# Three-layer graph network on one core: column chunks of 448, 448 and 458 behind the first pass, and two late bank drains in the plan

## The reference

```
gc(h, W, b) = adj @ (h @ W) + b
h  = maximum(layernorm(x), 0)
h  = relu(gc(h, W1, b1))        # W1 512 x 1024
h  = relu(gc(h, W2, b2))        # W2 1024 x 1024
out = x + gc(h, W3, b3)         # W3 1024 x 512
```

## Time and profile before

| what | us |
|---|---|
| median of 3 runs | 1581.48 |
| lowest and highest run | 1580.51 and 1583.2 |
| the profiled execution, its own time | 1582.09 |
| its span, first to last instruction | 1580.3 |
| PE busy | 1570.7 (99%) |
| DVE, ACT, POOL busy | 866.1, 644.3, 527.8 |
| mean granted clock of TensorE | 0.999 |

### The profile page before, as it was taken

The page is one execution under the profiler, slowest core; times in us unless marked ns, Lnnn a source line. Parts: engine busy times, 40 slices in busy tenths (PEclk is TensorE's granted clock), DMA queues, the critical chain, the costliest instruction groups (busy, mean ns, idle before and its releaser), DMA issues.

```text
span 1580.3 us, 21103 instructions
## 1 busy us (share of the span) xinstructions
PE 1570.7 (99%) x7638; PEld 1353.5 (86%) x7638; DVE 866.1 (55%) x1360; ACT 644.3 (41%) x1145; POOL 527.8 (33%) x488
## 2 busy tenths in 40 slices
PE   9999999999999999999999999999999999999999
PEld 7888889988878888989898989888898888888898
DVE  8983433256452456353545444764565536676766
ACT  5542222233343333342333333533455536555555
POOL 5863544346664544000000003573302333021302
PEclk9999999999999999999999999999999999999999
DMA  6966657555687888554557567783544357898887
GB/s 240 334 221 213 219 179 222 179 158 154 198 265 259 268 278 280 148 168 125 190 156 221 167 208 235 257 278 116 182 123 131 94 163 244 252 320 267 256 274 224
DMA packets 211091, 334.52 MB, mean 212 GB/s; under 512 B 25608, under 2 KB 96896, under 8 KB 210988
## 3 DMA queue, kind: packets, MB, share of 16 engines
q1 hardware_dynamic: 171484, 239.78, 49.1%
q0 software_dynamic: 15680, 55.31, 10.8%
q10 hardware_dynamic: 23824, 38.10, 6.9%
HBM read 243.75 MB, written 89.36 MB: 211 GB/s over the span
## 4 chain that ended last, share of the span: by engine, by line
PE 89%; DVE 4%; DMA 3%; ACT 2%; ACTq 1%; issue 0%; DVEq 0%; SPq 0%
PE ps L1818 29%; PE ps L1819 29%; PE ps L1820 29%; DVE ring L1449 2%; PE ps L1908 1%; PE ps L1907 1%; DMA raw<-adjT 1%; DMA raw<-HX 1%; DVE pair_buf L1491 1%; ACT pair_buf L1245 1%; DMA raw<-TS 1%; DVE even L1496 0%; ACT ring L1200 0%; DMA raw_tail<-adjX 0%; PE ps L1856 0%
## 5 line engine op out<-in xcount | busy, mean ns | idle before, releaser
L1449 DVE TENSOR_TENSOR ring<-raw,ring 128x512 fp32r<-128x512 f32 (+1 forms) x522 | 376.8, 738 | 409.6 <-ACT ring L1200 408.0
L1200 ACT CAST ring<-raw 128x512 fp32r<-128x512 f32 (+1 forms) x564 | 319.9, 576 | 489.4 <-PE ps L1820 373.4
L1818 PE MATMUL ps<-slots,still 128*128 128x512 f32 (+1 forms) x504 | 183.2, 364 | 1.5 <-DVE still L1397 1.0
L1819 PE MATMUL ps<-slots,still 128*128 128x512 f32 (+1 forms) x504 | 183.1, 363 | 0.0
L1820 PE MATMUL ps<-slots,still 128*128 128x512 f32 (+1 forms) x504 | 183.0, 363 | 0.0
L1818 PE MATMUL ps<-ring,even 128*128 128x512 f32 (+1 forms) x480 | 175.2, 365 | 2.5 <-DVE ring L1449 2.5
L1820 PE MATMUL ps<-ring,even 128*128 128x512 f32 (+1 forms) x480 | 175.0, 365 | 0.0
L1819 PE MATMUL ps<-ring,even 128*128 128x512 f32 (+1 forms) x480 | 174.9, 364 | 0.0
L1818 PE MATMUL ps<-ring,S 128*128 128x512 f32 (+1 forms) x420 | 153.1, 365 | 0.9 <-DVE ring L1449 0.9
L1819 PE MATMUL ps<-ring,S 128*128 128x512 f32 (+1 forms) x420 | 152.8, 364 | 0.0
L1820 PE MATMUL ps<-ring,S 128*128 128x512 f32 (+1 forms) x420 | 152.8, 364 | 0.0
(11 more groups left out here) (160 smaller groups left out, 3012.8 us busy)
## 6 DMA issues: line engine op xcount, KB each, us to landing
raw<-TS SPq DMA_DIRECT2D x160, 256.0 KB, 3.3
raw<-adjT SPq DMA_DIRECT2D x122, 256.0 KB, 3.9
raw<-adjT SPq DMA_DIRECT2D x41, 512.0 KB, 4.7
TS<-made SPq DMA_DIRECT2D x20, 1024.0 KB, 6.7
raw<-TS SPq DMA_DIRECT2D x80, 165.0 KB, 2.8
raw<-HS SPq DMA_DIRECT2D x50, 256.0 KB, 3.0
raw<-P SPq DMA_DIRECT2D x44, 256.0 KB, 4.2
HS<-pair_buf POOLq DMA_DIRECT2D x20, 512.0 KB, 4.8
```

The lines of the kernel that those rows point to most:

```text
L1200: act.copy(hi, src).then_inc(hi_done, 1)
L1449: dve.tensor_tensor(lo, src, hi.bitcast(F32), ALU.subtract).then_inc(lo_done, 1)
L1818: pe.matmul(out, st_hi, mv_hi, start=start, stop=False)
L1819: pe.matmul(out, st_hi, mv_lo, start=False, stop=False)
```

## The change

Two things are changed. First, `WIDTH` and `START` are doubled: the first pass keeps 512, 512 and 330 under the names `WIDTH1` and `START1`, with helpers `columns1`, `nodes1` and `within1`, and all later stages get 448, 448 and 458. Second, the planner puts off the "block" steps of the last two h1 blocks by 3 and 5 cuts instead of 2 (`LATE_BLOCKS`).

```diff
-WIDTH = (512, 512, 330)
-START = (0, 512, 1024)
+WIDTH1, WIDTH = (512, 512, 330), (448, 448, 458)
+START1, START = (0, 512, 1024), (0, 448, 896)
...
+LATE_BLOCKS = (3, 5)
...
-def columns_chunk(block):
+def columns_chunk(block, start):
...
-    return max(sum(c % HALF >= a for a in START) - 1 for c in range(first, last + 1))
+    return max(sum(c % HALF >= a for a in start) - 1 for c in range(first, last + 1))
...
-            p.later(lag, emit(g, j))
+            p.later({20: LATE_BLOCKS[0], 21: LATE_BLOCKS[1]}.get(j, lag), emit(g, j))
...
-            return slots1[:, j.slot, part, a, 0:WIDTH[c]]
+            return slots1[:, j.slot, part, a, 0:WIDTH1[c]]
...
+    def columns1(half, c):
+        return slice(half * STRIDE + START1[c], half * STRIDE + START1[c] + WIDTH1[c])
...
-                sp.dma_start(TS[t, :, :, within(c)], made[:, i % 2, :, 0:WIDTH[c]]).then_inc(made_stored[i % 2], 16)
+                sp.dma_start(TS[t, :, :, within1(c)], made[:, i % 2, :, 0:WIDTH1[c]]).then_inc(made_stored[i % 2], 16)
...
-                    need = columns_chunk(j.block) + 1
+                    need = columns_chunk(j.block, START1) + 1
...
-                    need = columns_chunk(j.block)
+                    need = columns_chunk(j.block, START)
```

More of the change, by code:

```diff
@@ L744, in slot1 @@
         if j.slot < RING1:
-            return slots1[:, j.slot, part, a, 0:WIDTH[c]]
-        return slots0[:, j.slot - RING1, part, a, 0:WIDTH[c]]
+            return slots1[:, j.slot, part, a, 0:WIDTH1[c]]
+        return slots0[:, j.slot - RING1, part, a, 0:WIDTH1[c]]
     def stage(s):
@@ L759, in within, with nodes1, within1 @@
         return slice(START[c], START[c] + WIDTH[c])
+    def columns1(half, c):
+        return slice(half * STRIDE + START1[c], half * STRIDE + START1[c] + WIDTH1[c])
+    def nodes1(half, c):
+        return slice(half * HALF + START1[c], half * HALF + START1[c] + WIDTH1[c])
+    def within1(c):
+        return slice(START1[c], START1[c] + WIDTH1[c])
     with ExitStack() as ctx:
@@ L950, in _ @@
                 if j.a is not None:
-                    src = adjT[j.block * P:(j.block + 1) * P, columns(j.a, j.chunk)]
-                    sp.dma_start(raw1[:, j.raw % RAW1, j.a, 0:WIDTH[j.chunk]], src)                         .then_inc(first_half_in if j.a == 0 else raw1_in[j.raw % RAW1], 16)
+                    src = adjT[j.block * P:(j.block + 1) * P, columns1(j.a, j.chunk)]
+                    sp.dma_start(raw1[:, j.raw % RAW1, j.a, 0:WIDTH1[j.chunk]], src)                         .then_inc(first_half_in if j.a == 0 else raw1_in[j.raw % RAW1], 16)
                     if j.a == 1:
@@ L962, in _ @@
                     for r in range(3):
-                        sp.dma_start(raw_tail[r * STEP:r * STEP + TAIL, :, 0:WIDTH[j.chunk]],
-                                     src[:, :, within(j.chunk)]).then_inc(tail1_in, 16)
+                        sp.dma_start(raw_tail[r * STEP:r * STEP + TAIL, :, 0:WIDTH1[j.chunk]],
+                                     src[:, :, within1(j.chunk)]).then_inc(tail1_in, 16)
                     continue
@@ L975, in _ @@
                     src = adjT[j.block * P:(j.block + 1) * P, :].rearrange("p (a n) -> p a n", a=2)
-                    sp.dma_start(raw1[:, r, :, 0:WIDTH[j.chunk]], src[:, :, within(j.chunk)]) \
+                    sp.dma_start(raw1[:, r, :, 0:WIDTH1[j.chunk]], src[:, :, within1(j.chunk)]) \
                         .then_inc(raw1_in[r], 16)
@@ L1124, in cut1 @@
             def cut1(j):
-                w = WIDTH[j.chunk] if j.chunk is not None else None
+                w = WIDTH1[j.chunk] if j.chunk is not None else None
                 if j.kind == "x":
@@ L1219, in _ @@
                             act.wait_ge(group_done, i + 1)
-                            act.copy(stage(s)[:, 0:WIDTH[c]], ps[:, 2 * m, 0:WIDTH[c]]).then_inc(copied, 1)
+                            act.copy(stage(s)[:, 0:WIDTH1[c]], ps[:, 2 * m, 0:WIDTH1[c]]).then_inc(copied, 1)
                             act.wait_ge(copied, 4 * c + m + 1)
@@ L1223, in _ @@
                             act.wait_ge(drained, 4 * c + m + 1)
-                        act.dma_start(P1[m, :, nodes(a, c)], stage(s)[:, 0:WIDTH[c]]) \
+                        act.dma_start(P1[m, :, nodes1(a, c)], stage(s)[:, 0:WIDTH1[c]]) \
                             .then_inc(stage_stored[s], 16)
@@ L1464, in _ @@
                     dve.wait_ge(group_done, i + 1)
-                    dve.tensor_copy(stage(s)[:, 0:WIDTH[c]], ps[:, 2 * m + 1, 0:WIDTH[c]]).then_inc(drained, 1)
+                    dve.tensor_copy(stage(s)[:, 0:WIDTH1[c]], ps[:, 2 * m + 1, 0:WIDTH1[c]]).then_inc(drained, 1)
             for kind, a in steps:
@@ L1585, in make @@
                 c, n = divmod(i, PAIRS)
-                w = WIDTH[c]
+                w = WIDTH1[c]
                 a, b = chunks1[c][2 * n], chunks1[c][2 * n + 1]
```

## The result

| | before | after |
|---|---|---|
| median, us | 1582.34 (4 runs) | 1597.8 (4 runs) |
| lowest and highest run | 1580.51 and 1584.9 | 1596.17 and 1599.19 |
| the profiled execution, its own time | 1582.09 | 1596.17 |
| its span | 1580.3 | 1594.4 |

The ratio is 1.0099, with a 95% interval from 1.0086 to 1.0112: slower by 15.5 us, where 5.5 us of gain were forecast. Of the rivals, 4 is the nearest.

What follows compares the result with a forecast made beforehand. PE, busy for 99% of the span, was taken as the bound. The terms 0 - 4.3 - 2.4 + 0.6 + 0.5 sum to -5.6 us, giving a forecast of 1576.0 us, own range 1574.5 to 1577.5.

Steps and rivals of the forecast that it cites:

- rival 4: The 448 lies off the straight line, a price step of 3.3 to 6.7 ns: 1587 to 1598 us; chance 0.05.
- Part 1: Matmuls of pass2, w2 and pass3, priced linearly by width: -90.4 and +90.6 us, together nothing within 0.5 us.
- rival 1: The 458 costs 3.3 ns more throughout, by the 330's dear pattern: +5.6 us, 1581.6; chance 0.09.
- Part 2: Pass2's begin: later drains remove PE's waits and the half clock, -4.6 us, leaving a 0.3 us wait: -4.3 us.
- Part 3: Pass3's last chunk: at 458 columns no waits on low parts and no dear 330 starts: -2.4 us.
- The cheaper pattern: Pass3's last chunk: the 458 at 203.9 ns, without the 3.3 ns extra of the 330 behind a wait.
- Part 4: First two chunks: shorter tiles cover loads less, 0.4 us in pass3, 0.2 in w2's first chunk: +0.6 us.
- Part 5: Kernel's end: the last DVE addition and store get 458 columns instead of 330: +0.5 us.
- Rivals 2 and 3: 2: loads not covered in narrower chunks, +2.5 us, chance 0.15; 3: late drains only move pass2's wait, +3 us, chance 0.05.

Runs made afterwards that it cites:

- the late drains alone: Against the kernel before, only the last two h1 blocks' later drains, all stages at 512, 512 and 330: 1578.97 us against 1581.91, ratio 0.9982.

## Why the prediction was wrong, step by step

**Part 1, the widths, "nothing within 0.5 us": wrong, and this is the failed step.** "I take the straight line, since two widths 182 columns apart lie on it with the same remainder" priced the 448 at 199.8 ns and the 458 at 203.9. They cost 202.7 and 208.3. Against before, the two chunks gain 3360 x (202.67 - 226.67) = -80.6 us, the third loses 1680 x (208.33 - 150.0) = +98.0, and the dear stretch adds 0.9: +18.2 (17.9 above was counted from the forecast's rounded prices). The bound named for the 448, 3.3 ns, held; the one for the 458, 3.3 ns too, did not (4.4). Two points always lie on a line, and their common remainder was no test of one. The rows had a warning in them, the 330's two prices 3.3 ns apart, which shows that the distance is set by something besides the columns; I used it for rival 1 and a chance of 0.05 for rival 4, though by my own count an error of 1 ns was 3.4 us, more than all that the change had to gain.

**Part 2, the late drains, -4.3: right in place and mechanism, too large.** The waits and the half clock went, and the rest of 0.3 us that I expected did not come: the first two chunks of pass2 lost 4.6 us in the profile before and lose nothing at their price in the late drains alone. Measured are -2.9 us with an interval of -4.3 to -1.4, and -3.3 at the new widths. I had taken one execution for all. In the four profiles of before these chunks lost 4.6, 3.8, 3.8 and 2.1 us, and by the clocks on record the 1.6 us of half clock is lost in about one execution in four.

**Part 3, the last chunk of pass3, -2.4: right for the waits.** 448 starts without one in 93.12 us, while with the late drains alone 1.0 us of waiting stays there. "The cheaper pattern" did not come into it, since the 458 has no price at 203.9.

**Part 4, less cover, +0.6: right in size, wrong in place.** The starts at 838.63 and 838.94 came 0.25 us late together, and four starts from 1398.11 to 1399.88 another 0.44, in the seventh part of pass3's first chunk: 0.7 us. The view of waits lists none of them, and the second profile of the changed kernel has them at the same places (837.64 and 1398.14). At the second place one of DVE's subtractions took 1.57 us instead of 0.62, beside a sum of POOL. In pass3's third part, where I expected 0.1 to 0.4 us, PE was not late; which link of that chain came sooner than I counted I did not follow up. That the size came out is luck. The 5.5 ns per KB came from one pair of medians; `raw<-adjT` of 165 and 256 KB landed in 3.6 and 3.9 us in the same trace, 3.3 ns per KB, and in the changed kernel the 224 KB of `TS` land in 3.3 us, no sooner than 256 KB did.

**Part 5, the end, +0.5: right.** From PE's last start at 1590.48 to the end of the span are 3.9 us, against 3.5: +0.4.

The first pass, which I took as the same, ran its 330 columns at 153.3 in the profiled execution after, so pass2 began at 438.43 and not at 436.65, 1.8 us later: the 1.6 us of chance above and starts 0.1 us late near 243.8. Together, for the profiled execution: 18.2 for the widths, 1.8 for the first pass and 0.1 for Part 4, less 0.3 for Part 2 and 0.1 for the end, are the 19.7 us.

**The rivals.** 4 is the nearest: the 448 is not on the line, at a distance over 202 ns. But it spoke of a step of 3.3 to 6.7 ns, worth 11 to 22 us, and the 448 is 2.9 ns high, 9.6 us, which alone would have given about 1586. That 1597.8 lies in its range of 1587 to 1598 is luck: the other 7.4 us are the 458's, and no rival had both widths off the line. The 458 is rival 1's place, with a price of its own and not with the 330's dear pattern. Rivals 2 and 3 did not come.

## What to carry to other kernels

Where PE is busy 99% of the time, price a new matmul width by a stream of that width alone, in the same data type; one sweep of about a millisecond gave twenty of them, true to the full kernels within 0.3 ns at the five widths that both have (330, 384, 448, 458 and 512), and two such prices in the kernel's own trace don't give the third. Of the three splits of 1354 float32r columns measured here, 512 + 512 + 330 is the cheapest, 603.4 ns for its three matmuls against 613.7 and 608.3. And a difference of 1.6 us, of the size of a pattern or one fall of the clock, is not to be read from a few profiles, while the granted clock of every execution says at once how often the clock fell.

## What the runs showed of the hardware that I had not expected

- The float32r matmul has an uneven price per width: 504 columns 226.7 ns like 512, and a remainder over columns / 2.4 from 12.5 ns (330) to 18.8 (456), where bfloat16 has 2.5 at the four widths measured.
- Some widths have two prices, 330 columns 150.0 or 153.3 ns, 448 columns 202.7 or 206.7. PE changed to the dear one within a chunk (near 243.8, 448.8 and 838.63) and then kept it for 200 to 490 matmuls; what brings the change is not shown.
- The granted clock falls to half behind some waits of TensorE and not behind others: behind 1.9, 2.06 and 2.12 us it did, behind 1.42, 1.84 and 2.35 it did not, and behind 2.37 and 3.52 us it did at one width and not at the other. The Trainium skill (TensorE: Matmul & The Clock Gate, "Why this matters for your kernels") warns of long idle gaps alone; the rows show falls behind shorter ones, and none behind a long one.
